# Keys' inputs loaded beside the last routed tiles, query and output weights loaded in another order, output products and row additions in other slots

## The chip, the cores and the metric

The program runs on one core of one Trainium2 chip. The metric is the device time of one execution in microseconds (us), lower is better. Three executions of the kernel before took 590.83, 594.02 and 596.88 us; the median is 594.02 us. The profile is of one more execution: 591.94 us, of which 590.1 us lie between the first and the last instruction (the span); 1.8 us lie around it.

## The reference

Four layers are added one after the other to `x` (4 x 256 tokens of 256 values, float32), each of the layer norm of the rows so far:

```python
x = x + _L0_xattn_ref(_layernorm(x), tokens, ctx, ctx, ctx)   # four experts, one for each token
x = x + _L0_ffn_ref(_layernorm(x), router_w, ...)             # 16 experts, 4 for each token, and a shared one
x = x + _L1_xattn_ref(_layernorm(x), ctx, seg, W_kvc, W_dq, W_uq, W_qr, W_uk, W_kr, W_uv, W_o)
x = x + _L1_ffn_ref(_layernorm(x), w_gate, w_up, w_down)      # 8-bit activations, ternary weights
```

The change lies between the second layer and the third. What the second leaves is, for each token, the sum of four rows (one for each chosen expert). The third is attention with compressed keys and queries:

```python
kv_c = kv @ W_kvc                 # 64 wide;  q_c = q @ W_dq is 96 wide
q_nope = q_c @ W_uq;  q_rope = rope(q_c @ W_qr)      # 16 heads
k_nope = kv_c @ W_uk; v = kv_c @ W_uv; k_rope = rope(kv_c @ W_kr)
attn = softmax(masked((q_nope . k_nope + q_rope . k_rope) * scale))
out = (attn @ v) @ W_o            # v @ W_o is folded into one product W_uv W_o for each head
```

## The kernel before

Everything is written out by hand: each engine has its own program (`@block.sync` for the DMA queue of SyncE, `gpsimd`, `scalar`, `tensor`, `vector`) and goes through it strictly in order; the engines meet at semaphores. A float32 product is split in three (`split3`, lines 413 to 415: high by high, low by high, high by low), so that nearly each result of TensorE in PSUM is copied by ScalarE into a high part (`copy`, L680), and VectorE then makes the low part (`lo`, L1567).

**Second layer, routed tiles.** 47 tiles of 128 slots each (`TILES`) are gathered, multiplied by their expert's weights and turned back; the loop over `j` runs on each engine. Tile `j`'s result is scaled by ScalarE into `yb` (three buffers; `slots_copy(j)`, L877, which waits until tile `j-3` has been stored) and stored to HBM by SP (`store_slots`, L493). At `j == 40` SP also issues the loads of `kr`, `uq`, `uk` and `qr`. Once tile 46 is stored, POOL gathers from HBM, four indirect DMAs for each tile of 128 tokens (`gather(t, k)`, L604), and VectorE adds the four into `X` (`combine(t)`, L2001 to L2003) and takes their mean and variance (`moments3`). POOL makes the reciprocal root (`power2`), VectorE the norm (`norm3`, L1578), TensorE turns it (`turn3`, L1065), ScalarE and VectorE split it (`hi_h`, `lo_h`), and `compress` makes `q_c` for a batch of 256 tokens.

**Preparation of the third layer.** `PREP` lists 14 units in the order in which every engine takes them: `kvT` (two, done early), `M` (two; 16 small products of `uq` and `uk` each), `K` (four; the keys from `kvT` and `kr`, then rotated by VectorE into `kA` and `kB`), `V` (two, transposes) and `VO` (four; eight products of `uv` and `wo` each). `prep_bank` gives each unit its PSUM bank. The units before `BEFORE` (all but `VO`) are done ahead of the loop over slots, those of `VO` at the slots that `BESIDES` names. `key_lo(n)` makes the low part of the keys, SP then swaps halves of the keys by DMA (`keys_swapped`).

**The loop over slots.** `PAIRS` = 32 pairs of heads (eight for each batch) go through a pipeline whose step is called slot `i`: TensorE takes `turn_p(i-4)`, `queries(i)`, `scores(i-2)`, then what is put beside (`BESIDES`), `values(i-4)`, `outputs(i-5)`; VectorE `lo_p(i-4)`, `rotate(i)` (L2046, L2048), `inverse(i-3)`, `masked(i-2)` (L2059), `lo_o(i-4)`, the units put beside, and at the slots in `COMBINE` `combine` and `moments3`; POOL `q_lo(i-1)`, `share01(i-3)`, `q_add(i)`, `power2`, and at the slots in `FETCH` one gather. `SIDE` puts two turns and one `compress` of the next batch at slots 4 to 6, 12 to 14 and 20 to 22. `quantise`, which is for the fourth layer, runs on VectorE at slots 15, 16, 23 and 24. The start of `rotate(i)` on VectorE is used below as the mark of slot `i`.

Of the kernel before, what the change touches and what calls it, by code (L numbers as in the profile page):

```python
# [16 lines left out]
P = 128  # L17
# [59 lines left out]
def build(nc, x_d, tok_d, seg_d, ctxT_d, router_d, gu_d, dn_d, kvc_d, dq_d, uq_d, uk_d, uv_d, qr_d, qrs_d,  # L77
# [6 lines left out]
    with ctx:  # L84
# [9 lines left out]
        def place(words, *groups):  # L94
# [3 lines left out]
            for n, group in enumerate(groups):  # L98
                scope = ExitStack()
                with scope:  # L100
                    for name, (shape, dt) in group.items():
# [82 lines left out]
                        "skip2": ([P, 512], F32), "uq": ([P, H, QC], F32), "uk": ([P, H, KVC], F32),  # L184
                        "qr": ([QC, NPAIR, 2 * R], F32), "skip3": ([P, 1048], F32), "wo": ([P, H, D], F32),
                        "qrs": ([QC, NPAIR, 2 * R], F32), "uv": ([P, H, KVC], F32)},
# [38 lines left out]
                       {"skip": ([P, 5120], F32), "kr": ([KVC, 4, P], F32), "kr_hi": ([KVC, 4, P], F32R),  # L225
                        "kr_lo": ([KVC, 4, P], F32R)},
                       {"skip": ([P, 5120], F32), "G_hi": ([P, KD, N], F32R), "G_lo": ([P, KD, N], F32R),
                        "yk": ([P, 2, TOPK, D], F32), "kvT_hi": ([KVC, N], F32R), "kvT_lo": ([KVC, N], F32R)},
# [87 lines left out]
        PREP = ([("kvT", n) for n in range(2)] + [("M", n) for n in range(2)]  # L316
                + [("K", n, ab) for n in range(2) for ab in range(2)]
                + [("V", x) for x in range(2)] + [("VO", n) for n in range(NPAIR // 2)])
# [4 lines left out]
        BESIDES = {0: (BEFORE, BEFORE + 1), 1: (BEFORE + 2, BEFORE + 3)}  # L323
# [19 lines left out]
        FETCH = {i: (4 + (i - 1) // TOPK, (i - 1) % TOPK) for i in range(1, 1 + 4 * TOPK)}  # L343
        COMBINE = {1: 2, 2: 3, 6: 4, 10: 5, 15: 6, 18: 7}
# [39 lines left out]
        def prep_bank(u):  # L384
            return (2, 3, 6, 7, 2, 3, 0, 1, 4, 5, 6, 7, 4, 5)[u]
# [33 lines left out]
        def _(sp):  # L419
# [75 lines left out]
            for j in range(TILES):  # L495
                store_slots(j)
                if j == 40:
                    sp.wait_ge(ternary_done_a, 3)
                    sp.dma_start(kr[:, :, :], kr_d).then_inc(kr_in, 16)
                    sp.dma_start(uq[:, :, :], uq_d).then_inc(uq_in, 16)  # L500
                    sp.dma_start(uk[:, :, :], uk_d).then_inc(uq_in, 16)
                    sp.dma_start(qr[:, :, :], qr_d).then_inc(uq_in, 16)
            sp.wait_ge(mask_g, 3 * NT)
            sp.dma_start(kvT_hi[:, :].bitcast(F32), kv_keep[0]).then_inc(kr_in, 16)
            sp.dma_start(kvT_lo[:, :].bitcast(F32), kv_keep[1]).then_inc(kr_in, 16)
            sp.dma_start(uv[:, :, :], uv_d).then_inc(wo_in[0], 16)
            sp.dma_start(wo[:, 0:NPAIR, :], wo_d[:, 0:NPAIR, :]).then_inc(wo_in[0], 16)
            sp.dma_start(wo[:, NPAIR:H, :], wo_d[:, NPAIR:H, :]).then_inc(wo_in[1], 16)
            sp.dma_start(qrs[:, :, :], qrs_d).then_inc(qrs_in, 16)
            for n in range(2):  # L510
# [15 lines left out]
        def _(pool):  # L526
# [93 lines left out]
            for k in range(3):  # L620
                gather(2, k)
            power2(1)
            gather(2, 3)
# [50 lines left out]
        def _(act):  # L674
# [4 lines left out]
            def copy(out, in_):  # L679
                return act.activation(out, in_, ACT.Copy)  # L680
# [201 lines left out]
            for j in range(TILES + 2):  # L882
# [14 lines left out]
                if j == 45:  # L897
                    act.wait_ge(kr_in, 16)
                    copy(kr_hi[:, :, :], kr[:, :, :]).then_inc(small_high_a, 1)
# [13 lines left out]
            for u in range(EARLY, BEFORE):  # L913
                prepare(u)
                if PREP[u] == ("M", 1):
                    copy(aq_hi[:, :, R:3 * R], qr[:, :, :])
# [5 lines left out]
            hi_h(1, 0, bank[4], G_hi)  # L922
# [4 lines left out]
            hi_h(1, 1, bank[5], G_hi)  # L927
            hi_q(0, bank[6][:, 0:S])
# [63 lines left out]
            for i in range(SLOTS):  # L992
# [17 lines left out]
                for u in BESIDES.get(i, ()):  # L1010
                    prepare(u)
# [50 lines left out]
        def _(pe):  # L1062
# [50 lines left out]
            def prepare(u):  # L1113
# [29 lines left out]
                else:  # L1143
                    pe.wait_ge(wo_in[0], 32)
                    if unit[1] >= 2:
                        pe.wait_ge(wo_in[1], 16)
# [203 lines left out]
            for t in range(TB):  # L1350
                turn3(NT + t, norm_v, None, norm_turned_p, bank[4 + t], hn2, 2)
            compress(0, bank[6][:, 0:S])
# [22 lines left out]
            def scores(i):  # L1375
                b_, r = i // NPAIR, i % 2
                pe.wait_ge(queries_low_g, i + 1)
                for h in range(2):
# [15 lines left out]
            def turn_p(i):  # L1394
                if i == 0:
                    pe.wait_ge(prep_read_v, NPREP)
# [70 lines left out]
            for i in range(SLOTS):  # L1467
# [6 lines left out]
                for u in BESIDES.get(i, ()):  # L1474
                    prepare(u)
# [81 lines left out]
        def _(dve):  # L1557
# [435 lines left out]
            dve.wait_ge(keys_table_in, 16)  # L1993
            for u in range(EARLY, VALUES):
                prepare(u)

# [27 lines left out]
            for n in range(2):  # L2024
                key_lo(n)
            link(dve.tensor_scalar(sin2[:, 0, :], sin1, upper[:, :], None, ALU.mult))
            dve.tensor_tensor(sin2[:, 1, :], sin1, sin2[:, 0, :], ALU.subtract)
            for u in range(VALUES, BEFORE):
                prepare(u)
# [5 lines left out]
            dve.wait_ge(small_high_a, 3)  # L2035
            lo(aq_lo[:, :, R:3 * R], qr[:, :, :], aq_hi[:, :, R:3 * R])
            lo_h(1, 1, bank[5], G_lo, G_hi)
            lo(bq_lo[:, :, :], qrs[:, :, :], bq_hi[:, :, :]).then_inc(small_low_v, 1)
            lo_q(0, bank[6][:, 0:S])
# [92 lines left out]
            for i in range(X3_LAG + NPAIR * (B - 1) + 1):  # L2132
# [26 lines left out]
                for u in BESIDES.get(i, ()):  # L2159
                    prepare(u)  # L2160
# [162 lines left out]
```

## Time and profile before

| what | value |
|---|---|
| median of three executions | 594.02 us (590.83 to 596.88) |
| profiled execution, and its span | 591.94 us, 590.1 us |
| busy: TensorE, VectorE, ScalarE, POOL | 501.4, 451.9, 357.2, 308.7 us |
| share of the chain that ended last: TensorE, VectorE, issue, ScalarE, DMA, POOL | 47%, 25%, 10%, 8%, 6%, 4% |
| mean granted clock of TensorE | 0.941 of full speed |
| last routed tile computed | about 262.4 us |
| first `combine` | 276.24 us |
| first `queries` | 289.25 us |
| last `rotate` (slot 31) | 478.84 us |

TensorE is the busiest engine, but not everywhere: the page's four slices from 251 to 310 us show it busy for 7, 6, 5 and 6 tenths, at a granted clock of 8, 5, 5 and 8 tenths. The chain that ended last is read as a list of what had to finish before what; "issue" is time in which an engine waited for nothing that the profile shows.

### The profile page before, as it was taken

To read this page: it belongs to the slowest core of one execution; us is meant where nothing else is said; L and a number is where in the kernel's file an instruction comes from. 1 tells how busy PE (TensorE), PEld (TensorE's weight loads), DVE (VectorE), ACT (ScalarE), POOL (GpSimd) and SP (SyncE) were. 2 spreads that over 40 slices of the span, in tenths; PEclk is the share of its full clock that TensorE was granted. 3 is DMA by queue.
4 is the path that set the end of the run, shared out by engine and by line. 5 is a ranking of instruction groups with operands and counts; after the bars stand their busy time and mean duration, and the time that the engine had idled before them with its cause. 6 is when DMAs were issued, how large, how long until landed. Compare 5 with 4: busy or idle time off the path is not lost.

```text
span 590.1 us, 11083 instructions
## 1 busy us (share of the span) xinstructions
PE 501.4 (85%) x3334; PEld 442.9 (75%) x3338; DVE 451.9 (77%) x1370; ACT 357.2 (61%) x903; POOL 308.7 (52%) x286
## 2 busy tenths in 40 slices
PE   0699978998899898976569999989998999588894
PEld 0588757777898787975359999989998998345673
DVE  4789947974878777736698889999998887759774
ACT  2354554253567677642237788857877889666543
POOL 2557660014478885315668787856665671362200
PEclk9999998999899999985588999989999999879998
DMA  7144443312364454568500000000000000000000
GB/s 271 53 124 140 154 117 110 81 61 64 106 195 145 150 187 107 127 200 294 142 19 19 19 29 27 21 18 1 3 1 2 2 1 2 0 1 1 19 27 27
DMA packets 27816, 45.24 MB, mean 77 GB/s; under 512 B 5680, under 2 KB 18832, under 8 KB 27120
## 3 DMA queue, kind: packets, MB, share of 16 engines
q1 hardware_dynamic: 20912, 28.15, 15.2%
q0 software_dynamic: 3792, 10.74, 7.1%
q10 hardware_dynamic: 3056, 5.65, 2.9%
q8 instruction: 29, 0.48, 0.3%
q14 instruction: 27, 0.22, 0.1%
HBM read 34.63 MB, written 8.85 MB: 74 GB/s over the span
## 4 chain that ended last, share of the span: by engine, by line
PE 47%; DVE 25%; issue 10%; ACT 8%; DMA 6%; POOL 4%; SPq 0%; ACTq 0%; DVEq 0%; another core or an unknown queue 0%; POOLq 0%
PE bank L1065 8%; PE bank L413 7%; PE bank L414 7%; PE bank L415 7%; PE bank L1508 5%; ACT pr L941 2%; DVE sc L2059 2%; PE bank L1266 2%; PE bank L1268 2%; PE bank L1267 2%; PE bank L1463 1%; DMA slots_y<-yb 1%; DVE X L1619 1%; DVE pT_lo L1567 1%; DMA bw<-bits_dram 1%
## 5 line engine op out<-in xcount | busy, mean ns | idle before, releaser
L576 POOL DMA_INDIRECT inb<-rows_kept,row_of x47 | 47.3, 1006 | 36.0 <-PE bank L1065 15.5
L941 ACT ACTIVATE pr<-sc,smin 128x256 f32<-128x256 f32 x128 | 63.3, 502 | 0.0
L648 POOL TENSOR_TENSOR Q_lo<-Q,Q_hi 128x512 fp32r<-128x512 f32 x32 | 41.5, 1297 | 27.7 <-ACT Q_hi L680 27.6
L634 POOL TENSOR_TENSOR pr<-pr,srec 128x512 f32<-128x512 f32 x32 | 33.3, 1041 | 29.6 <-DVE srec L2066 29.5
L2059 DVE CUSTOM_DVE_ANT_0 sc<-bank,bias 128x256 f32<-128x256 f32 x128 | 46.4, 418 | 0.0
L1567 DVE TENSOR_TENSOR pT_lo<-bank,pT_hi 128x512 fp32r<-128x512 f32 x64 | 41.2, 684 | 6.4 <-ACT pT_hi L680 6.4
L680 ACT ACTIVATE pT_hi<-bank 128x512 fp32r<-128x512 f32 x64 | 34.9, 596 | 14.6 <-PE bank L1065 14.1
L642 POOL TENSOR_TENSOR Q<-Q,rot 128x512 f32<-128x512 f32 x32 | 41.1, 1285 | 2.2 <-DVE Q L2048 2.2
L604 POOL DMA_INDIRECT yk<-slots_y,slot x32 | 33.1, 1035 | 16.7 <-DMA slots_y<-yb 6.7
L413 PE MATMUL bank<-pT_hi,V_hi 128*128 128x256 f32 x128 | 37.0, 289 | 4.7 <-DVE pT_lo L1567 4.7
L534 POOL TENSOR_TENSOR Wd<-wd_raw,Wd 128x512 fp32r<-128x512 f32 x13 | 16.9, 1298 | 45.0 <-ACT Wd L727 45.0
L950 ACT ACTIVATE pr<-pr,srec 128x256 f32<-128x256 f32 x64 | 29.1, 503 | 18.5 <-DVE srec L2066 18.5
L1065 PE MATMUL bank<-const,pr 128*128 128x128 f32 x256 | 34.7, 280 | 5.4 <-POOL pr L634 5.3
L413 PE MATMUL bank<-K_hi,Q_hi 128*128 128x256 f32 x128 | 37.1, 290 | 0.0
L415 PE MATMUL bank<-K_hi,Q_lo 128*128 128x256 f32 x128 | 36.8, 288 | 0.0
L414 PE MATMUL bank<-K_lo,Q_hi 128*128 128x256 f32 x128 | 36.8, 287 | 0.0
L415 PE MATMUL bank<-pT_hi,V_lo 128*128 128x256 f32 x128 | 36.6, 286 | 0.0
L414 PE MATMUL bank<-pT_lo,V_hi 128*128 128x256 f32 x128 | 36.5, 285 | 0.0
L1065 PEld LDWEIGHTS bank<-const,pr 128*128 128x128 f32 x256 | 29.7, 145 | 6.8 <-issue 3.6
L534 POOL TENSOR_TENSOR Wg<-wg_raw,Wg 128x512 fp32r<-128x512 f32 x22 | 28.2, 1296 | 11.0 <-ACT Wg L680 11.0
L877 ACT ACTIVATE yb<-bank,share 128x256 f32<-128x256 f32 x47 | 22.4, 476 | 15.6 <-PE bank L1292 9.0
L529 POOL TENSOR_TENSOR rstd<-vare,mhalf 128x1 f32<-128x1 f32 (+3 forms) x26 | 17.3, 667 | 27.3 <-DVE vare L1654 7.8
(340 smaller groups left out, 1952.9 us busy)
## 6 DMA issues: line engine op xcount, KB each, us to landing
slots_y<-yb SPq DMA_DIRECT2D x47, 128.0 KB
wg_raw<-gate_up_dram SPq DMA_DIRECT2D x22, 256.0 KB, 2.7
bw<-bits_dram ACTq DMA_DIRECT2D x3, 1024.0 KB
wd_raw<-down_dram SPq DMA_DIRECT2D x16, 128.0 KB
wo<-wo_dram SPq DMA_DIRECT2D x2, 1024.0 KB
wd_raw<-down_dram SPq DMA_DIRECT2D x30, 64.0 KB
gu_raw<-gate_up_dram SPq DMA_DIRECT2D x6, 256.0 KB, 3.4
X<-x_dram SPq DMA_DIRECT2D x2, 512.0 KB, 6.6
```

Of the source, the lines that this page charges most:

```text
L413: eng.matmul(out, w_hi, m_hi, start=first, stop=False, **kw)
L414: eng.matmul(out, w_hi, m_lo, start=False, stop=False, **kw)
L415: return eng.matmul(out, w_lo, m_hi, start=False, stop=last, **kw)
L534: return pool.tensor_tensor(out, in_, hi.bitcast(F32), ALU.subtract)
L576: pool.indirect_dma_start(inb[:, j % NIN, :], None, rows_d, bass.IndirectOffsetOnAxis(row_of[:, j:j + 1], 0)).then_inc(slots_in[j % NIN], 16)
L642: pool.tensor_tensor(Q[:, r, :], Q[:, r, :], rot[:, r, :, :].rearrange("p h s -> p (h s)"), ALU.add).then_inc(queries_summed_g, 1)
L648: pool.tensor_tensor(Q_lo[:, i % 2, :], Q[:, i % 2, :], Q_hi[:, i % 2, :].bitcast(F32), ALU.subtract).then_inc(queries_low_g, 1)
L680: return act.activation(out, in_, ACT.Copy)
L941: e = act.activation(pr[:, i % 2, z, :], sc[:, i % 2, z, :], ACT.Exp, bias=smin[:, i % 2, z:z + 1], scale=-1.0, accum_out=ssum[:, i % 2, z ...
L1065: return pe.transpose(out, in_, ident)
L1567: return dve.tensor_tensor(out, in_, hi.bitcast(F32), ALU.subtract)
L2059: dve.tensor_tensor_reduce(sc[:, r, z, :], bank[2 + h][:, u * S:(u + 1) * S], bias[:, TB * b_ + u, :], 1.0, 3.0e38, ALU.add, ALU.min, smin ...
```

## The change

- The third group of buffers moves: `kvT_hi`, `kvT_lo`, `kr`, `kr_hi`, `kr_lo` lie where weights of the first routed experts lay, and `uq` lies over buffers of the routed tiles, `uk` over weights of the last experts.
- SP issues `kr`, `kvT_hi` and `kvT_lo` after the stores of tiles 40, 41 and 42. ScalarE splits `kr` at `j == 45` only when all three have landed. `uq`, `uk`, `qr` and `qrs` are issued after the last store and the end of the last tile; `uv` and `wo` come in two halves, each after the four gathers of a tile (`gathered[n]`), and the swaps of the keys' halves after these.
- `PREP` has `K` and `V` ahead of `M`, in other banks. VectorE does all of them, with `key_lo`, `sin2` and the split of `qr`, before `combine(0)`; the split of `qrs` follows `moments3(0)`. ScalarE loads its table and splits `qrs` before the first `hi_h`.
- Two units of `VO` come between the first and the second turned tile, two at slots 0 and 1 (before: two at each). The first wait for all units moves from `turn_p(0)` to `scores(0)`.
- `COMBINE` moves from slots 1, 2, 6, 10, 15, 18 to 2, 3, 8, 11, 16, 19; `FETCH` begins at slot 3, not 1. One gather moves behind `power2(1)`.

```diff
--- before.py
+++ after.py
@@ -181,9 +181,10 @@
...
                         "skip": ([P, 2560], F32), "kA": ([P, 2, BANK], F32), "kB": ([P, 2, BANK], F32),
-                        "skip2": ([P, 512], F32), "uq": ([P, H, QC], F32), "uk": ([P, H, KVC], F32),
-                        "qr": ([QC, NPAIR, 2 * R], F32), "skip3": ([P, 1048], F32), "wo": ([P, H, D], F32),
-                        "qrs": ([QC, NPAIR, 2 * R], F32), "uv": ([P, H, KVC], F32)},
+                        "skip2": ([P, 512], F32), "kvT_hi": ([KVC, N], F32R), "kvT_lo": ([KVC, N], F32R),
+                        "kr": ([KVC, 4, P], F32), "kr_hi": ([KVC, 4, P], F32R), "kr_lo": ([KVC, 4, P], F32R),
+                        "qr": ([QC, NPAIR, 2 * R], F32), "wo": ([P, H, D], F32),
+                        "qrs": ([QC, NPAIR, 2 * R], F32), "uv": ([P, H, KVC], F32), "uk": ([P, H, KVC], F32)},
                        {"skip": ([P, ATT], F32),
@@ -222,10 +223,8 @@
...
                         "inb": ([P, NIN, ROWW], F32)},
-                       {"skip": ([P, 5120], F32), "kr": ([KVC, 4, P], F32), "kr_hi": ([KVC, 4, P], F32R),
-                        "kr_lo": ([KVC, 4, P], F32R)},
                        {"skip": ([P, 5120], F32), "G_hi": ([P, KD, N], F32R), "G_lo": ([P, KD, N], F32R),
-                        "yk": ([P, 2, TOPK, D], F32), "kvT_hi": ([KVC, N], F32R), "kvT_lo": ([KVC, N], F32R)},
+                        "yk": ([P, 2, TOPK, D], F32), "uq": ([P, H, QC], F32)},
                        {"skip": ([P, 11264], F32), "xr": ([P, NT, D], F32)}))
@@ -313,14 +312,13 @@
...
 
-        PREP = ([("kvT", n) for n in range(2)] + [("M", n) for n in range(2)]
-                + [("K", n, ab) for n in range(2) for ab in range(2)]
-                + [("V", x) for x in range(2)] + [("VO", n) for n in range(NPAIR // 2)])
+        PREP = ([("kvT", n) for n in range(2)] + [("K", n, ab) for n in range(2) for ab in range(2)]
+                + [("V", x) for x in range(2)] + [("M", n) for n in range(2)] + [("VO", n) for n in range(NPAIR // 2)])
         NPREP = len(PREP)
...
         BEFORE = PREP.index(("VO", 0))
-        BESIDES = {0: (BEFORE, BEFORE + 1), 1: (BEFORE + 2, BEFORE + 3)}
+        BESIDES = {0: BEFORE + 2, 1: BEFORE + 3}
         NCOPIED = [sum(w[0] != "K" for w in PREP[:u + 1]) for u in range(NPREP)]
@@ -340,8 +338,8 @@
...
         TERNARY = {4: 0, 15: 1, 26: 2}
-        FETCH = {i: (4 + (i - 1) // TOPK, (i - 1) % TOPK) for i in range(1, 1 + 4 * TOPK)}
-        COMBINE = {1: 2, 2: 3, 6: 4, 10: 5, 15: 6, 18: 7}
+        FETCH = {i: (4 + (i - 3) // TOPK, (i - 3) % TOPK) for i in range(3, 3 + 4 * TOPK)}
+        COMBINE = {2: 2, 3: 3, 8: 4, 11: 5, 16: 6, 19: 7}
         NORMS = [(2, 0), (2, 1), (2, 2), (2, 3), (2, 4), (2, 5), (3, 0), (3, 1), (2, 6), (2, 7), (3, 2), (3, 3), (3, 4),
@@ -382,7 +380,7 @@
...
         def prep_bank(u):
-            return (2, 3, 6, 7, 2, 3, 0, 1, 4, 5, 6, 7, 4, 5)[u]
+            return (2, 3, 2, 3, 0, 1, 4, 5, 6, 7, 6, 7, 2, 3)[u]
 
@@ -495,18 +493,24 @@
...
                 if j == 40:
-                    sp.wait_ge(ternary_done_a, 3)
                     sp.dma_start(kr[:, :, :], kr_d).then_inc(kr_in, 16)
-                    sp.dma_start(uq[:, :, :], uq_d).then_inc(uq_in, 16)
-                    sp.dma_start(uk[:, :, :], uk_d).then_inc(uq_in, 16)
-                    sp.dma_start(qr[:, :, :], qr_d).then_inc(uq_in, 16)
+                if j == 41:
+                    sp.dma_start(kvT_hi[:, :].bitcast(F32), kv_keep[0]).then_inc(kr_in, 16)
+                if j == 42:
+                    sp.dma_start(kvT_lo[:, :].bitcast(F32), kv_keep[1]).then_inc(kr_in, 16)
+            sp.wait_ge(slots_down_p, TILES)
+            sp.wait_ge(hidden_turned_p, TILES)
+            sp.wait_ge(slot_share_v, TILES)
             sp.wait_ge(mask_g, 3 * NT)
-            sp.dma_start(kvT_hi[:, :].bitcast(F32), kv_keep[0]).then_inc(kr_in, 16)
-            sp.dma_start(kvT_lo[:, :].bitcast(F32), kv_keep[1]).then_inc(kr_in, 16)
-            sp.dma_start(uv[:, :, :], uv_d).then_inc(wo_in[0], 16)
-            sp.dma_start(wo[:, 0:NPAIR, :], wo_d[:, 0:NPAIR, :]).then_inc(wo_in[0], 16)
-            sp.dma_start(wo[:, NPAIR:H, :], wo_d[:, NPAIR:H, :]).then_inc(wo_in[1], 16)
+            sp.dma_start(uq[:, :, :], uq_d).then_inc(uq_in, 16)
+            sp.dma_start(uk[:, :, :], uk_d).then_inc(uq_in, 16)
+            sp.dma_start(qr[:, :, :], qr_d).then_inc(uq_in, 16)
             sp.dma_start(qrs[:, :, :], qrs_d).then_inc(qrs_in, 16)
+            for n in range(2):
+                sp.wait_ge(gathered[n], 16 * TOPK)
+                heads = slice(n * NPAIR, (n + 1) * NPAIR)
+                sp.dma_start(uv[:, heads, :], uv_d[:, heads, :]).then_inc(wo_in[n], 16)
+                sp.dma_start(wo[:, heads, :], wo_d[:, heads, :]).then_inc(wo_in[n], 16)
             for n in range(2):
@@ -617,10 +621,11 @@
...
             power2(0)
-            for k in range(3):
+            for k in range(2):
                 gather(2, k)
             power2(1)
-            gather(2, 3)
+            for k in range(2, TOPK):
+                gather(2, k)
             for k in range(TOPK):
@@ -895,7 +900,7 @@
...
                 if j == 45:
-                    act.wait_ge(kr_in, 16)
+                    act.wait_ge(kr_in, 48)
                     copy(kr_hi[:, :, :], kr[:, :, :]).then_inc(small_high_a, 1)
@@ -913,19 +918,21 @@
...
                 if PREP[u] == ("M", 1):
-                    copy(aq_hi[:, :, R:3 * R], qr[:, :, :])
+                    copy(aq_hi[:, :, R:3 * R], qr[:, :, :]).then_inc(small_high_a, 1)
 
...
 
-            hi_h(1, 0, bank[4], G_hi)
             act.wait_ge(qrs_in, 16)
...
             act.activation(fo[:, :], mhalf[:, :], ACT.Exp)
-            hi_h(1, 1, bank[5], G_hi)
-            hi_q(0, bank[6][:, 0:S])
+            for t in range(TB):
+                hi_h(1, t, bank[4 + t], G_hi)
+            hi_q(0, bank[1][:, S:2 * S])
+            prepare(BEFORE)
+            prepare(BEFORE + 1)
 
@@ -1007,8 +1014,8 @@
...
                     hi_o(i - 4)
-                for u in BESIDES.get(i, ()):
-                    prepare(u)
+                if i in BESIDES:
+                    prepare(BESIDES[i])
                 if i == PAIRS + 4:
@@ -1141,9 +1148,7 @@
...
                 else:
-                    pe.wait_ge(wo_in[0], 32)
-                    if unit[1] >= 2:
-                        pe.wait_ge(wo_in[1], 16)
+                    pe.wait_ge(wo_in[unit[1] // 2], 32)
                     for x in range(4):
@@ -1347,9 +1352,11 @@
...
             pe.wait_ge(prep_read_v, BEFORE)
-            for t in range(TB):
-                turn3(NT + t, norm_v, None, norm_turned_p, bank[4 + t], hn2, 2)
-            compress(0, bank[6][:, 0:S])
+            turn3(NT, norm_v, None, norm_turned_p, bank[4], hn2, 2)
+            prepare(BEFORE)
+            prepare(BEFORE + 1)
+            turn3(NT + 1, norm_v, None, norm_turned_p, bank[5], hn2, 2)
+            compress(0, bank[1][:, S:2 * S])
             pe.wait_ge(small_low_v, 2)
@@ -1375,6 +1382,8 @@
...
                 pe.wait_ge(queries_low_g, i + 1)
+                if i == 0:
+                    pe.wait_ge(prep_read_v, NPREP)
                 for h in range(2):
@@ -1392,8 +1401,6 @@
...
             def turn_p(i):
-                if i == 0:
-                    pe.wait_ge(prep_read_v, NPREP)
                 for h in range(2):
@@ -1471,8 +1478,8 @@
...
                     scores(i - 2)
-                for u in BESIDES.get(i, ()):
-                    prepare(u)
+                if i in BESIDES:
+                    prepare(BESIDES[i])
                 if i == PAIRS + 3:
@@ -1991,8 +1998,17 @@
...
             dve.wait_ge(keys_table_in, 16)
+            dve.wait_ge(slots_down_p, TILES)
+            link(dve.tensor_scalar(sin2[:, 0, :], sin1, upper[:, :], None, ALU.mult))
+            dve.tensor_tensor(sin2[:, 1, :], sin1, sin2[:, 0, :], ALU.subtract)
             for u in range(EARLY, VALUES):
                 prepare(u)
+            for n in range(2):
+                key_lo(n)
+            for u in range(VALUES, BEFORE):
+                prepare(u)
+            dve.wait_ge(small_high_a, 3)
+            lo(aq_lo[:, :, R:3 * R], qr[:, :, :], aq_hi[:, :, R:3 * R])
 
@@ -2021,22 +2037,17 @@
...
             moments3(0)
-            for n in range(2):
-                key_lo(n)
-            link(dve.tensor_scalar(sin2[:, 0, :], sin1, upper[:, :], None, ALU.mult))
-            dve.tensor_tensor(sin2[:, 1, :], sin1, sin2[:, 0, :], ALU.subtract)
-            for u in range(VALUES, BEFORE):
-                prepare(u)
+            dve.wait_ge(small_high_a, 4)
+            lo(bq_lo[:, :, :], qrs[:, :, :], bq_hi[:, :, :]).then_inc(small_low_v, 1)
             norm3(0)
...
             norm3(1)
-            dve.wait_ge(small_high_a, 3)
-            lo(aq_lo[:, :, R:3 * R], qr[:, :, :], aq_hi[:, :, R:3 * R])
             lo_h(1, 1, bank[5], G_lo, G_hi)
-            lo(bq_lo[:, :, :], qrs[:, :, :], bq_hi[:, :, :]).then_inc(small_low_v, 1)
-            lo_q(0, bank[6][:, 0:S])
+            lo_q(0, bank[1][:, S:2 * S])
+            prepare(BEFORE)
+            prepare(BEFORE + 1)
 
@@ -2156,8 +2167,8 @@
...
                     lo_o(i - 4)
-                for u in BESIDES.get(i, ()):
-                    prepare(u)
+                if i in BESIDES:
+                    prepare(BESIDES[i])
                 if i in COMBINE:
```

## Rows read from the trace of the kernel before

**Rows 1.** Busy time by stretch: us, engines PE, PEld, DVE, ACT, POOL, clock, DMA, GB/s.
```profile
262.00:276.00 14.00, 12.69 (x62) 11.01 (x61) 5.56 (x10) 4.19 (x9) 7.57 (x8) 0.50 0.85 291
```
**Rows 2.** Chain that ended last, in order of time: start us, us, what.
```profile
253.68 6.17 DMA slots_y<-yb
...
269.14 6.92 DMA yk<-slots_y,slot
```
**Rows 3.** Timeline of ScalarE: start us, us, line, operation [idle before, releaser].
```profile
255.32 0.62 ACT L680 ACTIVATE kr_hi<-kr 64x512 fp32r<-64x512 f32 x1
...
262.46 0.47 ACT L877 ACTIVATE yb<-bank,share 128x256 f32<-128x256 f32 x1 [1.72 <-PE bank L1292]
...
268.07 1.05 ACT L680 ACTIVATE aq_hi<-qr 96x1024 fp32r<-96x1024 f32 x1
```
**Rows 4.** Timeline of the queue of SP.
```profile
263.83 0.60 SPq L505 DMA_DIRECT2D kvT_lo<-kv_keep  x1
```
**Rows 5.** DMA issues, whole span and 235 to 300: size, median us to landing.
```profile
wg_raw<-gate_up_dram SPq DMA_DIRECT2D x22, 256.0 KB, 2.7
...
qr<-qr_dram SPq DMA_DIRECT2D x1, 384.0 KB, 7.5
...
qrs<-qrs_dram SPq DMA_DIRECT2D x1, 384.0 KB, 13.3
```
**Rows 6.** Timeline of TensorE: M, the first K, second turn, queries(0), first VO.
```profile
262.22 5.27 PE L1142 MATMUL bank<-uk,uq 128*96 128x64 f32 x32
...
268.19 0.79 PE L413 MATMUL bank<-kvT_hi,kr_hi 64*128 64x512 f32 x1 [0.70 <-DMA kvT_lo<-kv_keep]
...
285.02 0.69 PE L1065 MATMUL bank<-const,hn 128*128 128x128 f32 x2 [3.05 <-DVE hn L1578]
...
289.25 0.55 PE L413 MATMUL bank<-q_hi,aq_hi 96*128 96x256 f32 x1 [1.01 <-DVE q_lo L1567]
...
291.44 3.52 PE L1149 MATMUL bank<-wo,uv 128*64 128x256 f32 x16
```
**Rows 7.** Timeline of VectorE, 276 to 305: combine(0), keys, norm3(0), combine(2), combine(3).
```profile
276.24 0.69 DVE L2001 TENSOR_TENSOR yk<-yk 128x512 f32<-128x512 f32 x1 [1.10 <-DMA yk<-slots_y,slot]
...
278.63 1.28 DVE L1700 SCALAR_TENSOR_TENSOR K_lo<-kA,K_hi 128x512 fp32r<-128x512 f32 x2
...
280.56 0.60 DVE L1578 TENSOR_SCALAR hn<-X,mv,rstd 128x256 f32<-128x256 f32 x1
...
284.89 1.21 DVE L1567 TENSOR_TENSOR aq_lo<-qr,aq_hi 96x1024 fp32r<-96x1024 f32 x1
...
299.51 0.69 DVE L2001 TENSOR_TENSOR yk<-yk 128x512 f32<-128x512 f32 x1
...
304.49 1.85 DVE L2001 TENSOR_TENSOR yk<-yk 128x512 f32<-128x512 f32 x1
```
**Rows 8.** Timeline of POOL: first gather in a slot, first share.
```profile
302.26 0.97 POOL L604 DMA_INDIRECT yk<-slots_y,slot  x1 [3.17 <-DVE vare L2008]
...
309.49 1.04 POOL L634 TENSOR_TENSOR pr<-pr,srec 128x512 f32<-128x512 f32 x1
```
**Rows 9.** Timeline of VectorE: rotate at slots 6, 7, 8, 10, 12, 14, 15.
```profile
326.02 0.68 DVE L2046 TENSOR_TENSOR rot<-bank,sin 128x512 f32<-128x512 f32 x1
...
333.53 0.68 DVE L2046 TENSOR_TENSOR rot<-bank,sin 128x512 f32<-128x512 f32 x1
...
339.05 0.68 DVE L2046 TENSOR_TENSOR rot<-bank,sin 128x512 f32<-128x512 f32 x1
...
350.15 0.68 DVE L2046 TENSOR_TENSOR rot<-bank,sin 128x512 f32<-128x512 f32 x1
...
362.39 0.68 DVE L2046 TENSOR_TENSOR rot<-bank,sin 128x512 f32<-128x512 f32 x1
...
374.12 0.68 DVE L2046 TENSOR_TENSOR rot<-bank,sin 128x512 f32<-128x512 f32 x1
...
380.35 0.68 DVE L2046 TENSOR_TENSOR rot<-bank,sin 128x512 f32<-128x512 f32 x1
```

## The prediction

> **What bounds the kernel now.** I read the chain that ended last, then the timelines of all engines between 250 and 330 us, then the spacing of slots. Outside that stretch the change only shifts a few VectorE operations, so everything is decided there. The seam between the layers is a relay. First comes the queue: tile 41's store, issued behind `kr`, `uq`, `uk` and `qr`, holds ScalarE until 259.6, and the next link is 6.92 us, a gather waiting behind the attention weights [rows 2]. Between 262 and 276 TensorE is busy 12.7 of 14 us, at half clock [rows 1], but on nothing that is waited for; what ends the wait is the gather, and `combine(0)` starts at 276.24. From there to `queries(0)` at 289.25 are 13.0 us of norm, turn, split and compress [rows 6, 7]. Then the slots fill. Their pace is 5.52 us (slots 7 to 8 [rows 9]), but slots 0 to 6 take much longer, VectorE carrying two combines in them.
>
> **The tail of the routed tiles.** 1664 KB leave the queue ahead of tile 41's store; 512 KB of `kvT` come in their stead, behind the stores of tiles 41 and 42. The stall on that store goes. What is late next is `kvT_lo`: ScalarE's split of `kr` ran at 255.32 without a wait [rows 3] and now needs it. It is issued after tile 42's store, at about 254.05. A load of 256 KB took 2.7 us to land [rows 5]; the same `kvT_lo`, issued at 263.83 in a full queue, released TensorE at 268.19, 4.4 us later [rows 4, 6]. So it lands between 256.8 and 258.4; I take 257.5, as the queue is then half full. Behind this wait on ScalarE stand the SiLU of tile 46 and the copies of tiles 45 and 46. From the split to the end of the last product I count 4.0 us (split, SiLU, hidden, turn, two splits, five products): 261.5 in place of 262.4. Gain 0.9 us, bounds 3.1 (no wait) and nothing.
>
> **Keys first, then M.** K (12 products) and V then take TensorE until about 268.5, and VectorE and ScalarE follow close; before, M did so from 262.22 [rows 6]. M now needs `uq`, `uk`, `qr`, which leave only when the last tile is stored: issued at 262.4, 263.0 and 263.5. `qr` took 7.5 us to land behind the other two [rows 5], which gives 271.0, and I add 0.2 for the gathers. Behind M stands VectorE's whole queue, `combine(0)` first. Before, from M's start to the end of ScalarE's `aq_hi<-qr` (268.07 + 1.05) passed 6.9 us [rows 3, 6]; with VectorE's 1.21 us for `aq_lo` [rows 7] that is 8.2. So `combine(0)` starts at 271.2 + 8.2 = 279.4, **3.2 us later** than 276.24. The gathers of tile 0, issued from 264.4 on with less ahead of them, are hidden under it: even 6.92 us after the last issue they are in by 275. Bounds: if `qr` lands 6 us after issue and the tail gives 3.1, no delay, since the gathers hold `combine(0)` until about 276; if `qr` takes the 13.3 us that `qrs` took with twice as much ahead [rows 5], 8.8 us.
>
> Row and rule on the clock: TensorE was at 0.50 for the whole stretch from 262 to 276, though busy 91% of it [rows 1], and I keep M at that half level. The Trainium skill (TensorE: Matmul & The Clock Gate, What's actually happening) says that sustained activity brings the clock up; by it M would take half its 5.3 us, and the total would be 2.6 us less. The row contradicts it for just these products.
>
> **From combine(0) to queries(0).** Keys' low parts (1.28 us) and `sin2`, 1.9 us from 278.63 to 280.56, leave VectorE's path; `bq_lo` takes their place, 1.21 like `aq_lo` [rows 7]. One gather less stands ahead of `power2(1)`, 0.3. So the second norm is ready 1.0 us sooner, at 7.3 after `combine(0)`. But 16 products of VO now stand between the turns; at half clock 16 took 3.52 us [rows 6]. The first turn ends 5.1 after `combine(0)`, so the second starts at 8.6 against 8.8 (285.02 less 276.24). Gain 0.2 us; 1.3 if the VO products lift the clock for `compress`, a loss of 0.8 if `wo`'s first half is late. It is issued once tile 0's gathers are in, needs some 5 us, and VO asks for it at 284.5. The keys' swaps go out after tile 1's gathers, near 278; scores(0) asks for them past 300.
>
> **Slots 0 to 6.** From `queries(0)` to `rotate(6)` pass 36.8 us [rows 6, 9]. Eight VO products less before `queries(1)` give 1.2 us at `rotate(1)`. Before, `combine(2)` stood ahead of `rotate(2)`, and `combine(3)` ahead of `rotate(3)` and so of the first share, which POOL began at 309.49, 20.2 us after `queries(0)` [rows 6, 8]. POOL's gather in slot 1 waited 3.17 us for `combine(2)`, ahead of `q_lo(1)` [rows 8]. Now one combine stands ahead of the share, not two: 2.4 us less (0.69 for its first addition, 1.7 for the rest). The first addition of `combine(3)` took 1.85 us, not 0.69 [rows 7], while POOL added `Q`. That is VectorE and POOL holding each other up. The Trainium skill (SBUF — State Buffer, SBUF: two separate sides) has them exclude one another on a shared pair of ports; by it the new `combine(2)` can be hit likewise, and the gain is 1.2 us less. My step by step working puts the share near 15.7 after `queries(0)`; `combine(3)` behind it delays `lo_p(0)` by about 0.4. Gain 4.1 us, bounds 2.4 and 5.2.
>
> **Later slots.** Slot 6, with a compress and a combine, took 7.51 us; with a compress alone (slot 14) 6.23 [rows 9]: 1.3 less. A combine alone costs 1.2 over two slots: slots 10 and 11 took 12.24 against 11.04 [rows 9]. That is what slot 8 gets. Slots 11 for 10, 16 for 15 and 19 for 18 move a combine beside a turn or a second quantise, where VectorE cannot catch up in the next slot; I take 0.2 each, bounds nothing and 0.7. Together +0.5, bounds -0.1 and +2.0. The gathers start two slots later and so do the norms that need them; each keeps a slot, over 5 us, before its combine, where VectorE would stand if it did not.
>
> **The sum.** +3.2 - 0.2 - 4.1 + 0.5 = -0.6 us (the tail's 0.9 is in the 3.2): 591.3 us for the profiled execution of 591.94. That one is 2.1 us under the median of 594.02; against the median I predict 593.4 us. Three runs spread over 6 us, about 1%, which is what a measurement of this kernel can tell from no change.
>
> **Rivals.**
> - Faster: the weights come quickly. If `kr`'s split hardly waits and `qr` lands 6 us after issue at most, `combine(0)` is back at 276.2, where gathers hold it; with 4.8 in the slots and 1.3 before them the time is 594.0 + 0 - 1.3 - 4.8 - 0.1 = 587.8 us. For it: at the 291 GB/s that the queues moved [rows 1] the three loads, 1.7 MB, need 5.8 us from 262.4 on. Against it: 7.5 us measured for the same load, and nothing suggests a faster path. Chance 0.17.
> - M at the upper clock level (half of its 5.27 us [rows 6]): 2.6 us less, 590.8. Within 1% too; chance 0.08.
> - Slower: M becomes the bound that the gathers share in. If the gathers of two tiles and the four loads hold one another back so that `qr` needs what `qrs` needed, the delay is 8.8 us, and with 3.1 in the slots the end is 594.0 + 8.8 - 0.2 - 3.1 + 0.5 = 600.0 us. It turns slower than before once `qr` lands more than 8.3 us after its issue (7.7 in the forecast, and the 0.6 us gained), and slower by 1% near 13. For it: 6.92 us for a gather in such a queue [rows 2]. Against it: only 2.1 MB are queued, not 3.4. Chance 0.15.
> - The change hides nothing: VectorE could have added tile 0's rows while waiting for M, and does not, so what slots win is only given back ahead of them. That is the forecast itself, near 593 to 594. Chance 0.60.
>
> **Numbers.** The forecast has 0.60 and a range of its own of 590 to 597; the clock rival's 0.08 falls within 1% too (588.1 to 600.0). The slower rival's price lies at that edge, so 0.02 of its 0.15 stay within. Faster by over 1%: 0.17; within: 0.70; slower by over 1%: 0.13. The range for 8 in 10 goes from 587.0 to 599.2: it takes in the faster rival's price and nearly the slower one's, and leaves out about 0.1 on each side.
>
> **What would show it.** The split of `kr` on ScalarE after a wait for `kvT_lo`, near 257.5. K before M on TensorE, M starting on a DMA at about 271 at half clock, and an idle gap before it. `combine(0)` at 279.4 released by no gather but by VectorE's own `aq_lo`. `queries(0)` at 292, the first share 15.7 after it, `rotate(6)` 32.7 after it, near 325. Slot 6 at 6.2 us. Wrong would be: M at 267 or 275; a stall of VO for `wo`; a combine that waits for its gather at slot 11 or 19; a first share later than 18 after `queries(0)`.

## The result and the profile after

The changed kernel takes 597.66 us (median of 20 runs, 592.71 to 604.58), the kernel before 593.49 us beside it (20 runs). The ratio, of fast runs alone, is 1.0059, 95% interval 1.0038 to 1.0080: 3.5 us slower. The forecast was 0.6 us faster; the time lies in the range of 587.0 to 599.2, the sign is wrong.

The profiled execution has a span of 593.2 us, 3.1 more than before. The two profiles also differ ahead of the change and in the last layer, so the stages are compared from a mark ahead of the change, the SiLU of tile 45 (254.14 us before, 255.56 after). Timeline of ScalarE in the changed kernel: start us, us, line, operation [idle before, releaser].

```profile
255.56 0.32 ACT L868 ACTIVATE sil<-bank 128x176 f32<-128x176 f32 x1 [0.48 <-PE bank L1273]
...
258.92 0.63 ACT L685 ACTIVATE kr_hi<-kr 64x512 fp32r<-64x512 f32 x1 [2.08 <-DMA kvT_lo<-kv_keep]
...
263.08 0.47 ACT L882 ACTIVATE yb<-bank,share 128x256 f32<-128x256 f32 x1 [0.73 <-PE bank L1297]
...
278.53 1.05 ACT L685 ACTIVATE aq_hi<-qr 96x1024 fp32r<-96x1024 f32 x1
```

These answer to [rows 3]: the split of `kr` now waits 2.08 us. TensorE, for [rows 6]:

```profile
262.98 0.79 PE L411 MATMUL bank<-kvT_hi,kr_hi 64*128 64x512 f32 x1
...
272.52 5.38 PE L1149 MATMUL bank<-uk,uq 128*96 128x64 f32 x32 [2.35 <-DMA qr<-qr_dram]
...
285.98 3.68 PE L1154 MATMUL bank<-wo,uv 128*64 128x256 f32 x16
289.59 0.69 PE L1072 MATMUL bank<-const,hn 128*128 128x128 f32 x2
...
293.17 0.36 PE L411 MATMUL bank<-q_hi,aq_hi 96*128 96x256 f32 x1 [1.02 <-DVE q_lo L1574]
```

K runs first, then TensorE idles 2.35 us until `qr` has landed, and M takes 5.38 us at a granted clock of 0.50. VectorE, for [rows 7]; slot 3 stands at the end:

```profile
279.61 1.22 DVE L1574 TENSOR_TENSOR aq_lo<-qr,aq_hi 96x1024 fp32r<-96x1024 f32 x1 [0.19 <-ACT aq_hi L685]
280.76 0.68 DVE L2017 TENSOR_TENSOR yk<-yk 128x512 f32<-128x512 f32 x1
...
303.91 1.34 DVE L2017 TENSOR_TENSOR yk<-yk 128x512 f32<-128x512 f32 x1
...
310.61 1.55 DVE L2017 TENSOR_TENSOR yk<-yk 128x512 f32<-128x512 f32 x1
...
313.88 1.59 DVE L1585 TENSOR_SCALAR hn<-X,mv,rstd 128x256 f32<-128x256 f32 x1
315.38 1.28 DVE L1574 TENSOR_TENSOR pT_lo<-bank,pT_hi 128x512 fp32r<-128x512 f32 x2
316.58 0.67 DVE L2057 TENSOR_TENSOR rot<-bank,sin 128x512 f32<-128x512 f32 x1
```

`combine(0)` waits for no gather, only for `aq_lo`; the combine in slot 3 and the norm behind it, both longer than elsewhere (1.55 and 1.59 us), stand ahead of `lo_p(0)` (the row at 315.38) and `rotate(4)` (316.58). POOL's first share, for [rows 8]:

```profile
309.35 1.04 POOL L639 TENSOR_TENSOR pr<-pr,srec 128x512 f32<-128x512 f32 x1 [2.51 <-DVE srec L2077]
```

And `rotate` at slots 6, 10, 11, 12, 13, 14 and 31, for [rows 9] (timeline of VectorE):

```profile
327.43 0.68 DVE L2057 TENSOR_TENSOR rot<-bank,sin 128x512 f32<-128x512 f32 x1
...
351.45 0.68 DVE L2057 TENSOR_TENSOR rot<-bank,sin 128x512 f32<-128x512 f32 x1
...
357.00 0.68 DVE L2057 TENSOR_TENSOR rot<-bank,sin 128x512 f32<-128x512 f32 x1
...
365.03 0.67 DVE L2057 TENSOR_TENSOR rot<-bank,sin 128x512 f32<-128x512 f32 x1
...
371.49 0.68 DVE L2057 TENSOR_TENSOR rot<-bank,sin 128x512 f32<-128x512 f32 x1
...
376.78 0.68 DVE L2057 TENSOR_TENSOR rot<-bank,sin 128x512 f32<-128x512 f32 x1
...
483.34 0.68 DVE L2057 TENSOR_TENSOR rot<-bank,sin 128x512 f32<-128x512 f32 x1
```

Slot 11, from one `rotate` to the next, lasts 8.03 us, slot 12 6.46 (before: 6.44): nothing is won back there. Stage by stage, in us:

| stage | before | after | difference | forecast |
|---|---|---|---|---|
| SiLU of tile 45 to `combine(0)` | 22.1 | 25.2 | +3.1 | +3.2 |
| `combine(0)` to `queries(0)` | 13.0 | 12.4 | -0.6 | -0.2 |
| `queries(0)` to `rotate(6)` | 36.8 | 34.3 | -2.5 | -4.1 |
| `rotate(6)` to `rotate(31)` | 152.8 | 155.9 | +3.1 | +0.5 |
| sum | | | +3.1 | -0.6 |

Outside these stages the two profiles differ by +1.4 us ahead and -1.4 us behind (111.3 and 109.9 us from `rotate(31)` to the end; the twelve profiles below have 111.0 to 113.0), so these cancel.

### The profile page after: what moved, and what is told of

Its sections match the earlier page's. It is cut to its first block, busy times and chain, and to the rows that moved or that the text cites. A ratio compares the mean times of both kernels' runs of the same rounds, so it can differ in the third digit from the quotient of the medians.

```text
span 593.2 us, 11088 instructions
## 1 busy us (share of the span) xinstructions
PE 501.5 (85%) x3338; PEld 440.5 (74%) x3338; DVE 454.7 (77%) x1370; ACT 357.1 (60%) x903; POOL 309.6 (52%) x286
## 4 chain that ended last, share of the span: by engine, by line
PE 44%; DVE 27%; issue 11%; ACT 8%; DMA 5%; POOL 4%; SPq 1%; DVEq 0%; ACTq 0%; POOLq 0%
PE bank L1072 7%; PE bank L411 6%; PE bank L412 6%; PE bank L413 6%; PE bank L1515 4%; ACT pr L948 2%; DVE sc L2070 2%; DVE pT_lo L1574 2%; PE bank L1271 2%; PE bank L1273 2%; PE bank L1272 2%; PE bank L1470 1%; DVE X L1626 1%; POOL pr L639 1%; DMA seg<-seg_dram 1%
## 5 line engine op out<-in xcount | busy, mean ns | idle before, releaser
L1271 PE MATMUL bank<-Wg,xT_hi 128*128 x94 | 31.2, 332 | 0.0
```

The lines of the kernel that those rows point to most:

```text
L1271: pe.matmul(out, xT_hi[:, j % 3, k, :], hi, start=(k == 0), stop=False)
```

## The experiments

Ratios are to the kernel before, run beside each; 95% interval in brackets. The intervals of the single edits overlap that of the changed kernel (1.0038 to 1.0080), so what one edit is worth is read in its profile as much as in its ratio; only the runs with several edits stand clear of it. The edits are shown shortened, with remarks of mine; in profiles a stage counts from the same mark, the SiLU of tile 45. Theory A was that late combines ahead of a turn and the early ones' loss in slot 3 make up the difference; its rivals stand with each run.

**late_back**
```diff
-COMBINE = {2: 2, 3: 3, 8: 4, 11: 5, 16: 6, 19: 7}    # gathers from slot 3
+COMBINE = {2: 2, 3: 3, 8: 4, 10: 5, 15: 6, 18: 7}    # gathers from slot 2
```


> The changed kernel with the combines of tiles 5, 6 and 7 back at slots 10, 15 and 18 (and the gathers one slot earlier, at slots 2 to 17); all else as changed. Theory A (a combine directly ahead of a slot that turns, or beside the second quantise, costs its full 2.4 us, since VectorE has no spare time in the next slot to win it back): rotate(10) to rotate(14) shrinks from 25.3 to 24.0 us, rotate(18) to rotate(22) from 25.3 to 24.0, rotate(15) to rotate(18) from 21.8 to 21.3; together 3.2 us less than the changed kernel, which brings it to about the time of the kernel before (ratio 1.000 to 1.002). Rival B (the loss against before lies ahead of slot 6, in the later combine(0), and these slots differ by chance between two profiles): the spacing of these slots stays as in the changed kernel and the ratio stays at 1.005 to 1.006.

Ratio 1.0037 [1.0008, 1.0066]. Slots 10 to 14 took 24.2 us, 18 to 22 24.0, as expected; but slots 15 to 18 22.7, since slot 16 took 8.07. That does not follow from the slots of the combines: slot 16 took 8.08 or 8.09 in four more runs below and 6.70 in two with combines in the same late slots. Slot 3 rose to 9.81 and slot 2 fell to 5.63 (changed: 8.67 and 6.58), so the moved gather costs 0.2 us there. Theory A's spacing holds for slots 10 to 14 and 18 to 22; the ratio, whose interval holds both theories' numbers, decides nothing.

**late_alone**
```diff
-COMBINE = {1: 2, 2: 3, 6: 4, 10: 5, 15: 6, 18: 7}    # kernel before; gathers from slot 1
+COMBINE = {1: 2, 2: 3, 8: 4, 11: 5, 16: 6, 19: 7}    # gathers from slot 3
```


> The kernel before with only the late combines moved, tiles 4 to 7 to slots 8, 11, 16 and 19, and the gathers to slots 3 to 18. Theory A: slots 10 to 14 and 18 to 22 each 1.35 us longer, 15 to 18 0.5 us longer, slots 6 to 10 0.1 shorter: 3.1 us slower than before, ratio 1.005, nearly the whole loss of the full change. Rival B: within 0.1% of before, ratio 0.999 to 1.001. The gathers no longer wait for combine(2) at slot 1, which may give up to 1 us back near slot 2.

Ratio 1.0044 [1.0014, 1.0073]: 2.6 us, by this edit alone. From `rotate(6)` to `rotate(31)` 155.9 us (before 152.8), slot 11 8.02 and slot 19 8.02. From `queries(0)` to `rotate(6)` it also took 0.7 us more than before, where up to 1 us back was expected. Rival B is out. Timeline of VectorE, `rotate(11)` and `rotate(12)`:

```profile
355.59 0.68 DVE L2046 TENSOR_TENSOR rot<-bank,sin 128x512 f32<-128x512 f32 x1
...
363.61 0.68 DVE L2046 TENSOR_TENSOR rot<-bank,sin 128x512 f32<-128x512 f32 x1
```

Between them lies slot 11, which took 8.02 us with the combine in it. It holds the norm of tile 4 too (`norm3(4)`, which VectorE takes ahead of `rotate(12)`); the kernel before has the combine in slot 10 and the norm in slot 11.

**kr_apart**
```diff
-act.wait_ge(kr_in, 48)        # kr, kvT_hi, kvT_lo
+act.wait_ge(kr_in, 16)        # kr; TensorE waits for kvT on a semaphore of its own
```


> The changed kernel with ScalarE's split of kr waiting for kr alone; kvT is counted on another semaphore, for which only TensorE waits. Theory A: the 2.08 us wait on kvT_lo is on the path (last tile, then the weights' loads, then M, then combine(0)), so the last product ends, uq is issued, M starts and combine(0) starts 1.5 to 2.1 us sooner: ratio against before 1.002 to 1.003 in place of 1.006. Rival B (M is held by the transfer rate with the gathers in the same queues): the last tile ends sooner but combine(0) by less than 0.5 us, ratio unchanged.

Ratio 1.0027 [0.9999, 1.0055], 1.9 us under the changed kernel. ScalarE splits `kr` with no wait, and `combine(0)` comes 22.7 us after the mark, not 25.2:

```profile
258.61 0.62 ACT L685 ACTIVATE kr_hi<-kr 64x512 fp32r<-64x512 f32 x1
259.20 0.32 ACT L868 ACTIVATE sil<-bank 128x176 f32<-128x176 f32 x1
```

That is 2.5 us sooner; theory A had 1.5 to 2.1, B less than 0.5. The wait was on the path.

**rows_first**
```diff
+combine(0)
+moments3(0)
 for u in (M0, M1): prepare(u)
+norm3(0)
 lo(aq_lo, qr, aq_hi)
-combine(0)
-moments3(0)
 lo(bq_lo, qrs, bq_hi)
-norm3(0)
 combine(1)
```


> The changed kernel with VectorE adding tile 0's rows (combine(0) and its moments) before it splits M, and the split of qr behind norm3(0). Theory A (combine(0) waits only because VectorE takes M's splits and aq_lo first; the gathers of tile 0 are in by 275.4, when SP issues uv): combine(0) starts near 275.5 in place of 280.8. M's last split then comes at 278.7 to 279.4 and norm3(0) behind it, and tile 1's gathers are in at about 281.1, so that combine(1) starts near 281.5 in place of 285.2 and queries(0) is 3 to 3.7 us sooner: ratio against before 0.999 to 1.001. Rival B (what the front gains is taken back because tile 1's gathers or wo's first half come late): queries(0) less than 1 us sooner, ratio 1.004 or more.

Ratio 1.0023 [0.9994, 1.0053], 2.1 us under the changed kernel. `combine(0)` is now released by its gather:

```profile
277.69 0.69 DVE L2015 TENSOR_TENSOR yk<-yk 128x512 f32<-128x512 f32 x1 [3.74 <-DMA yk<-slots_y,slot]
```

From the mark (257.85) `queries(0)` comes after 34.4 us, 3.2 sooner, as A said; at `rotate(6)` 1.6 are left, and the ratio stays above A's 0.999 to 1.001. The stretches of 5 us from 290 (busy time by engine, then TensorE's clock) show what differs, this run first, the changed kernel second:

```profile
290.00:295.00 5.00, 3.98 (x19) 3.25 (x20) 2.25 (x4) 1.35 (x3) 3.78 (x5) 0.50 0.75 184
295.00:300.00 5.00, 5.00 (x25) 3.16 (x21) 2.82 (x5) 1.23 (x2) 2.69 (x3) 0.50 0.39 123
```

```profile
290.00:295.00 5.00, 3.05 (x17) 2.40 (x15) 2.23 (x4) 1.74 (x4) 3.78 (x5) 0.84 0.60 157
295.00:300.00 5.00, 4.34 (x27) 2.43 (x26) 3.28 (x6) 1.82 (x3) 3.46 (x3) 0.80 0.41 116
```

The first slots ran at 1.2 GHz up to 300 us, in the changed kernel mostly at 2.4: slots 0 and 1 took 4.12 and 3.99 us, not 3.46 and 2.71. That the edit lowers the clock is not shown: `rows_back` below, which has the changed kernel's code up to `queries(0)`, was granted 0.77 and 0.50 in these stretches.

**rows_back**
```diff
-COMBINE = {2: 2, 3: 3, 8: 4, 11: 5, 16: 6, 19: 7}    # gathers from slot 3
+COMBINE = {1: 2, 2: 3, 6: 4, 10: 5, 15: 6, 18: 7}    # gathers from slot 1
```


> The changed kernel with all six moved combines and the gathers back in their old slots (1, 2, 6, 10, 15, 18; gathers at 1 to 16); loads, order of K, V, M and VO as changed. Theory A (moving the combines costs more in the late slots than it gives in the early ones): rotate(6) to rotate(31) is back at 152.8 us (changed: 155.9). The early move gave 4.1 us at the first share but VectorE then lost 2.1 us behind it in slot 3, so from queries(0) to rotate(6) I expect 35 to 36 us (changed 34.3, before 36.8): 1.5 to 2.5 us less than the changed kernel in all, ratio against before 1.002 to 1.003. Rival B (the early move is worth its full 4 us, since the front is a relay): queries(0) to rotate(6) 38 us, ratio 1.006 to 1.007, no better than the changed kernel.

Ratio 1.0054 [1.0019, 1.0088], as the changed kernel; the interval holds both theories' numbers. `queries(0)` to `rotate(6)` took 36.9 us, 2.7 more than in the changed kernel. But 1.0 of the 2.7 lies ahead of `rotate(1)`, where neither kernel has a combine and this one ran at the lower clock, so the early move is worth 1.7 us at most by this pair. Other pairs give 1.3 (`early_alone` against the kernel before), 0.4 (`best1_qr` against `three_qr`) and -1.2 (`best1` against `all_three`): its worth is open. The late slots took 154.3, of which 1.4 are slot 16's 8.09. With all combines back the loss stays: over the whole kernel the moves about cancel, and what remains is the later `combine(0)`, 25.6 us after the mark here.

**early_alone**
```diff
-COMBINE = {1: 2, 2: 3, 6: 4, 10: 5, 15: 6, 18: 7}    # kernel before; gathers from slot 1
+COMBINE = {2: 2, 3: 3, 6: 4, 10: 5, 15: 6, 18: 7}    # gathers from slot 2
```


> The kernel before with only combine(2) and combine(3) moved, to slots 2 and 3, and the gathers to slots 2 to 17; late combines and all else as before. Theory A: queries(0) to rotate(6) falls from 36.8 to about 35 us (two VO units in slots 0 and 1 still hold the start), slots 6 to 31 stay at 152.8, or 0.5 to 1.5 more where a gather now stands in slot 16 beside quantise: ratio 0.997 to 1.001. Rival B (full worth of the early move): 33 us, ratio 0.993 to 0.995.

Ratio 1.0012 [0.9975, 1.0049]: no gain that can be measured. 35.5 us from `queries(0)` to `rotate(6)`, 1.3 less than before, 0.6 of it in slot 0, which has no combine in either; slot 3 took 9.80.

**qr_early**
```diff
 if j == 43:
+    sp.dma_start(qr, qr_d).then_inc(uq_in, 16)       # no longer behind uk
```


> The changed kernel with the load of qr (384 KB) issued after tile 43's store, so that only uq and uk stand between the last store and M. Theory A (M, and with it combine(0), is held by these loads): from uq's issue to M's start 7.1 us in place of 8.4; combine(0) and queries(0) 1.3 us sooner; ratio against before 1.003 to 1.004 in place of 1.006. Rival B (M waits for uq or for the gathers in the queue, not for what stands last): M starts at most 0.4 us sooner, ratio unchanged.

Ratio 1.0036 [1.0004, 1.0068], 1.4 us under the changed kernel. M starts 6.6 us after `uq`'s issue, not 8.4, and waits for `uk`:

```profile
270.26 5.38 PE L1150 MATMUL bank<-uk,uq 128*96 128x64 f32 x32 [0.82 <-DMA uk<-uk_dram]
```

`combine(0)` comes 24.2 us after the mark, 1.0 sooner, and `queries(0)` 1.3 sooner; at `rotate(6)` nothing is left of it in this profile, which was granted 0.50 from 295 to 300 us. The loads behind the last tile hold M, and M holds `combine(0)`.

**vo_back**
```diff
-BESIDES = {0: BEFORE + 2, 1: BEFORE + 3}             # two units between the turns
+BESIDES = {0: (BEFORE, BEFORE + 1), 1: (BEFORE + 2, BEFORE + 3)}
```


> The changed kernel with all four VO units back at slots 0 and 1, two each (their banks stay as changed, and scores(0) still waits for all of them). Theory A: VO between the turns cost the second turn 0.9 us (its norm was ready at 288.7, it began at 289.6), but freed slots 0 and 1: queries(0) comes 0.5 to 0.9 us sooner, and queries(0) to rotate(3) is 1.2 to 1.6 us longer; in all 0.3 to 1.1 us slower than the changed kernel, ratio 1.0065 to 1.0075. Rival B (without VO ahead of it TensorE enters slot 0 at the lower clock level as in the kernel before, and pays there): 2 us or more slower, ratio 1.009 or more.

Ratio 1.0122 [1.0078, 1.0166], six runs: VO between the turns is a gain. The ratio is rival B's, not A's, and `queries(0)` came 0.5 us later where A had it sooner; TensorE was granted 0.50 from 290 to 295, not 0.84. But the profile accounts for less than B's 2 us: `queries(0)` to `rotate(6)` 0.9 us longer and `combine(0)` 0.6 later, which no edit explains. So the sign is shown, the size is not.

**best1, best1_qr, all_three, three_qr** take the edits together: `best1` is late_back with kr_apart and rows_first, `all_three` has rows_back in place of late_back, and `_qr` adds qr_early.

> The changed kernel with three edits together: late combines at 10, 15, 18 (as in the run late_back), ScalarE's split of kr waiting for kr alone (as in kr_apart), and tile 0's rows added before M's splits (as in rows_first). If the three add up, 1.3 + 1.9 + 2.1 = 5.3 us less than the changed kernel: ratio against before 0.997. Rival (two edits of the front work on the same relay, and TensorE at half clock takes part of it back, as it did in rows_first): 3 to 4 us less, ratio 0.999 to 1.001.

> As best1, but all combines and gathers in their old slots (as in rows_back). Theory A: against best1 the early slots lose 1 us and the late ones gain 1 to 1.5 (no gather beside quantise in slots 16 and 17): ratio 0.996 to 0.999. Rival B (full worth of the early move): 2 to 3 us slower than best1, ratio 1.001 to 1.003.

> best1 with qr's early load. Where tile 0's rows are added first, combine(0) waits for its gathers, which share the queues with the loads: M starts 1.3 us sooner, the gathers land up to 1 us sooner, and norm3(0) follows M's splits. Theory A: 1 us less than best1, ratio 0.994 to 0.996. Rival B (gathers set the pace and do not gain): the same as best1, 0.996 to 0.997.

> all_three with qr's early load. Theory A: 1 us less than all_three, ratio 0.994 to 0.996. Rival B: the same as all_three, 0.996 to 0.997.

| run | ratio | 95% interval | median us | before us |
|---|---|---|---|---|
| best1 | 0.9963 | 0.9933 to 0.9993 | 591.65 | 593.71 |
| all_three | 0.9966 | 0.9932 to 1.0001 | 591.34 | 593.71 |
| best1_qr | 0.9946 | 0.9917 to 0.9975 | 589.94 | 593.14 |
| three_qr | 0.9920 | 0.9889 to 0.9951 | 588.83 | 593.14 |

The edits add up (1.3 + 1.9 + 2.1 us expected 0.997). The early load adds 1.0 us to `best1`, as A said, and 2.7 to `all_three`, more than either theory had; the intervals overlap. `three_qr` is the fastest, below both kernels, with M at 6.1 us after `uq`'s issue. The slots of the combines make no difference that can be measured between `best1` and `all_three`; neither has the late slots of the changed kernel.

## Why the prediction was wrong

**The tail: right.** The split waited until 3.5 us after `kvT_lo`'s issue, as taken (257.5 less 254.05). `kr_apart`, without the wait, is about 2 us faster; the prediction had 2.2 for it (a gain of 3.1 without the wait, 0.9 with it).

**M and `combine(0)`: right.** 8.4 us from `uq`'s issue to M, forecast 8.8; M at the half level for 5.38 us; `combine(0)` right behind `aq_lo`, +3.1 against +3.2. In the four profiles with this front it comes 25.2 to 25.8 us after the mark, in the three with the old one 21.7 to 22.1, so the typical figure is nearer +3.7. qr_early and rows_first each take part of it away. The rule by which TensorE should have run faster under M (the Trainium skill, TensorE: Matmul & The Clock Gate, What's actually happening) was rightly set aside for M, busy 5.38 of 5.50 us at 0.50. VO's products ran at 0.50 too, but right behind them the trace agrees with the rule: 0.50 from 288 to 290, 0.93 from 290 to 291 and 1.00 after it. `compress` ran at the upper level, and `queries(0)` came 0.4 us nearer to `combine(0)` than forecast.

**Slots 0 to 6: mis-sized.** The share was as forecast (16.2 us after `queries(0)`, 15.7 expected). The new `combine(2)` was hit by POOL, as the prediction allowed (1.2 us less gain): two of its additions took 1.34 us for 0.68 (at 303.91) and 1.37 for 0.42 (at 305.74). What failed is "`combine(3)` behind it delays `lo_p(0)` by about 0.4": from the share to `rotate(4)` passed 7.2 us, before 5.1 (309.49 to 314.57), so 2.1 us were given back. I had the bare durations; in the trace the addition took 1.55 for 0.68 and the norm 1.59 for 0.41, each while POOL added or subtracted. -2.5 instead of -4.1 lies at the lower bound.

**Later slots: the largest miss.** What failed is "I take 0.2 each, bounds nothing and 0.7". Measured are +1.36 (slots 10 to 13: 25.33 against 23.97), +0.5 and +1.34: 3.2 for 0.6. The first and the third came in every run with combines at 11 and 19 (1.3 to 1.5); the middle one did not: slots 15 to 18 took 21.0 to 21.8 us there, and 21.3 or 22.7 with the combine at 15.

Only the next slot's 0.5 us of catching up was counted as lost. But a combine, 2.4 us of VectorE's work, costs 1.1 us of time at slot 8, since VectorE is busy for only 4.48 us of a plain slot of 5.55 and has room in its own slot and the next. In slot 11 it meets the norm of tile 4:

```profile
363.00 0.91 DVE L1585 TENSOR_SCALAR hn<-X,mv,rstd 128x256 f32<-128x256 f32 x1
...
369.29 0.41 DVE L1585 TENSOR_SCALAR hn<-X,mv,rstd 128x256 f32<-128x256 f32 x1 [0.83 <-POOL rstd L533]
```

So slot 11 took 2.5 us more than a plain one (VectorE busy 7.45 of 8.03), and slot 12, with a turn, gave nothing back. Before, slot 12 had TensorE busy for all of its 6.44 us, VectorE for 5.80. In the changed kernel VectorE is busy for 5.63 of 6.46 there, and stands for 0.83 waiting for POOL's reciprocal root of the rows just added, which the norm of tile 5 needs (the second row). This wait is there at slots 12 and 20 in every run with combines at 11 and 19, `late_alone` too, and in no other. The prediction's "each keeps a slot, over 5 us, before its combine" looked at the gathers and not at what comes after the combine. Which of the two, TensorE's full slot or the wait for POOL, keeps slot 12 from giving back was not tried. `late_alone` shows the cost of the late combines by itself: 2.6 of the 3.5 us measured. Slot 6 (6.25) and slots 8 and 9 (+1.1) came as forecast.

**The sum and the chances.** Of the 3.7 us between +3.1 and -0.6, the later slots make 2.6, slots 0 to 6 1.6, and the stretches ahead of them take 0.5 back. Either of the two misses alone would have turned the sign. A loss of 0.6% lies within the 1% that had 0.70. The slower rival named the wrong place, though: `qr` did not need the 13 us of `qrs` but 6.9, and no rival put the loss in the late slots, though their upper bound of 0.7 each should have been asked what it excluded.

## What to carry to other kernels

When work moves between steps of a pipeline, ask of each new neighbour how full the engine is there: work costs little where the engine has room in that step and the next, and all of its duration where it meets other added work and the next step has no room. Ask also who waits for its result, and how soon. When inputs are reordered, the consumer that is first in an in-order engine sets the pace of everything behind it; here VectorE added ready rows only after it had waited for weights. A wait for several loads is worth splitting by who needs which.

## What was not expected of the hardware

- TensorE's level at the start of the slots goes with more than a microsecond: 0.84 and 0.80 granted from 290 to 295 and 295 to 300 us in the changed kernel, 0.50 and 0.50 in `rows_first`, where slots 0 and 1 took 1.9 us more. It differs also between kernels with the same code up to there (`rows_back`: 0.77 and 0.50, `late_back`: 0.67 and 0.68), so a difference of 1 or 2 us in this stretch between two single profiles shows little of an edit.
- With a combine in slot 15, slot 16 takes 6.70 or 8.09 us in kernels with the same instructions there. The timelines of VectorE and POOL in late_back, a long case:

```profile
399.14 0.35 DVE L2113 TENSOR_SCALAR xr<-hn,xrec 128x256 f32<-128x256 f32 x1
399.53 1.84 DVE L2116 TENSOR_SCALAR xr<-xr 128x256 f32<-128x256 f32 x1
```

```profile
399.93 1.29 POOL L653 TENSOR_TENSOR Q_lo<-Q,Q_hi 128x512 fp32r<-128x512 f32 x1
```

The second step takes 1.84 us and ends as POOL's subtraction does (401.37, 401.22); in the kernel before the same step took 0.46, and POOL's `Q_lo` began 0.19 us after its end, not 0.40 after its start. In all five long cases POOL's subtraction began 0.39 or 0.40 us after the step's start, in all three short ones 0.58 to 0.65: a shift of a few tenths of a microsecond goes with which it is. That was not tried by itself: what shifts it is open.
